# Constant rows of the attention tiles written by ScalarE and VectorE, all attention roots on VectorE, the score bound finished in thirds

## The reference

```
h = concat(tok(x), txt(x_txt))
h = h + ssm(layernorm(h))       # long convolution, gelu, linear, gelu, norm
h = h + ffn(layernorm(h))       # the last stage, the one that is changed
```

```
sx = x @ hl_w + hl_b ; q, k, v = linear maps of sx
att = softmax(q k^T * 4 + causal)               # for each n, e
mixed = sum_e gate_e * (att @ v) + resid        # gate: softmax of a linear map
hn = layernorm(mixed)                           # 36 groups of 16 per partition
hx = relu(fc1(hn)) ; hx = fc2(hx) ; y = layernorm(hx + hn)
out = y * softmax(y @ fgate)
```

## Time and profile before

| | us |
|---|---|
| time, median of 3 runs (lowest to highest) | 1520.96 (1516.12 to 1527.62) |
| the profiled execution's own time | 1521.13 |
| its span in the profile | 1519.4 |
| PE busy | 1209.2 (80%) |
| PEld busy | 612.7 (40%) |
| DVE busy | 823.8 (54%) |
| ACT busy | 830.5 (55%) |
| POOL busy | 379.0 (25%) |

### The profile page before, as it was taken

One profiled execution on the slowest core, in us unless ns is written; L12 is line 12 of the kernel. 1 busy time (PEld: TensorE's weight loads), 2 busy tenths in 40 slices (PEclk: granted clock), 3 DMA queues, 4 the chain that ended last, 5 costly groups with the idle time before them and its releaser, 6 DMA issues.

```text
span 1519.4 us, 28823 instructions
## 1 busy us (share of the span) xinstructions
PE 1209.2 (80%) x11006; PEld 612.7 (40%) x11103; DVE 823.8 (54%) x1727; ACT 830.5 (55%) x1050; POOL 379.0 (25%) x606
## 2 busy tenths in 40 slices
PE   4895558880507998899899989889989988999963
PEld 2462257760203543343343344334334434433421
DVE  4844973357622363556457457445745744654345
ACT  0231034440205587667758758766875876777750
POOL 2000040022003221432432423243242324323410
PEclk9997779995558999999999999999999999999985
DMA  9999179703139007404701910740380192065000
GB/s 158 184 186 181 14 169 202 155 1 75 49 114 135 1 13 135 64 13 88 118 1 60 134 25 14 130 76 13 79 127 1 36 140 43 13 113 86 1 17 9
DMA packets 121632, 120.66 MB, mean 79 GB/s; under 512 B 73762, under 2 KB 90417, under 8 KB 121215
## 3 DMA queue, kind: packets, MB, share of 16 engines
q1 hardware_dynamic: 117449, 118.29, 42.8%
q10 hardware_dynamic: 3733, 0.60, 0.3%
q0 software_dynamic: 320, 0.04, 0.0%
HBM read 91.05 MB, written 22.95 MB: 75 GB/s over the span
## 4 chain that ended last, share of the span: by engine, by line
PE 36%; issue 8%; ACT 8%; DMA 7%; SPq 5%; DVE 5%; POOL 5%; POOLq 0%; ACTq 0%; DVEq 0%
PE b_pso L1988 13%; PE b_pss L1964 10%; ACT b_pb L2098 7%; POOL b_stat L2121 3%; DMA qk_parts_b<-b_qs 3%; PE b_psm L2015 3%; DMA b_qop<-bound_part 3%; PE b_psm L2031 2%; PE b_psm L2045 2%; DMA b_ot<-in_c_ones 2%; POOL b_pb L2140 2%; SPq L1871 1%; PE b_psm L1947 1%; SPq L1903 1%; SPq L1904 1%
## 5 line engine op out<-in xcount | busy, mean ns | idle before, releaser
L2098 ACT ACTIVATE b_pb<-b_pss 128x1024 f32<-128x1024 f32 (+2 forms) x736 | 660.1, 934 | 334.5 <-PE b_pss L1964 255.0
L2140 POOL TENSOR_SCALAR_AFFINE_SELECT b_pb<-b_pb 128x256 f32<-128x256 f32 (+1 forms) x544 | 224.6, 431 | 719.9 <-ACT b_pb L2098 714.0
L1988 PE MATMUL b_pso<-b_pb,b_vop 128*32 128x77 f32 (+4 forms) x5376 | 375.9, 386 | 34.9 <-POOL b_pb L2140 32.7
L1964 PE MATMUL b_pss<-b_qop,b_kop 128*128 128x512 bf16 (+3 forms) x1439 | 321.7, 329 | 78.5 <-issue 53.8
L1964 PEld LDWEIGHTS b_pss<-b_qop,b_kop 128*128 128x128 bf16 x1536 | 125.0, 101 | 257.2 <-issue 108.3
L1988 PEld LDWEIGHTS b_pso<-b_pb,b_vop 128*32 128x32 f32 x5376 | 113.6, 110 | 211.7 <-issue 167.9
L2306 DVE TENSOR_TENSOR b_ofm<-b_pso,b_mk 128x512 f32<-128x512 f32 (+1 forms) x96 | 51.6, 538 | 158.2 <-PE b_pso L1988 157.3
L918 PE MATMUL psc<-tz,ub 128*64 128x128 f32 x1152 | 80.2, 284 | 45.5 <-DVE tz L1030 36.6
L2188 DVE COPY b_ot<-b_psm 128x336 f32<-128x336 f32 (+1 forms) x96 | 40.0, 417 | 104.5 <-PE b_psm L2015 104.3
L2121 POOL TENSOR_TENSOR b_stat<-b_stat,b_mh 128x18 f32<-128x18 f32 x30 | 96.0, 3216 | 0.0
L918 PEld LDWEIGHTS psc<-tz,ub 128*64 128x64 f32 x1152 | 72.0, 142 | 53.4 <-DVE ub L1026 34.2
(11 more groups left out here) (404 smaller groups left out, 1466.4 us busy)
## 6 DMA issues: line engine op xcount, KB each, us to landing
b_qop<-qk_parts_b SPq DMA_DIRECT2D x192, 144.0 KB
tz<-taps SPq DMA_DIRECT2D x64, 304.0 KB, 9.7
x<-in_x SPq DMA_DIRECT2D x16, 1024.0 KB, 13.7
qk_parts_b<-b_qs SPq DMA_DIRECT2D x16, 864.0 KB, 5.6
b_kop<-qk_parts_b SPq DMA_DIRECT2D x192, 36.0 KB
b_mk<-b_mskf SPq DMA_DIRECT2D x128, 36.0 KB, 4.9
qk_parts_b<-b_ks SPq DMA_DIRECT2D x8, 432.0 KB, 4.0
n_late<-id_d SPq DMA_DIRECT2D x1, 2400.0 KB, 9.4
```

The costliest lines, as they stand in the source:

```text
L1964: mm = pe.matmul(pss[:, u % 2, b, col:col + w], lhs, qop[:, n, e, q0:q0 + w], start=True, stop=True, skip_group_check=True)
L1988: mm = pe.matmul(pso[VW * ee:VW * (ee + 1), (3 * n + x) % 2, q0 - QT * x:q0 - QT * x + w], vop[0:r, j, n, :], pb[0:r, slot_, b, cc:cc + w] ...
L2098: nc.scalar.activation(pb[:, s % PB, 0:nb, 0:w], pss[:, s % 2, 0:nb, 0:w], ACT.Exp, scale=float(HD) ** 0.5).then_inc(exped, 1)
L2140: ins = pool.affine_select(out=v_, in_=v_, compare_op=ALU.is_ge, fill=0.0, base=0, pattern=pat, channel_multiplier=-1)
```

## The change

The constant rows. SP's 13 transfers are gone, and with them the four constants in DRAM. VectorE writes three numbers into a small tile `kons`, first thing in the stage. ScalarE copies them, broadcast along the row and read as pairs of bf16: zeros into rows 96 to 127 of head 0 of `qop` and of `kop` before its first split (`early_consts`), and after its last split of period -1 the row of -1 in `kop`, ones in all of `mk`, and the zeros of heads 1 to 3 of `qop` (`late_consts`). Each copy counts `late_ok` up by one, to 7. SP waits for the count that belongs to a head before it places that head's bound row and mask. VectorE writes the rows of `fxt`, `hx1`, `pm` and `ot` by memsets at steps 46, 49, 52 and 14 of period 0.

The roots. POOL's `root` is gone. VectorE runs `inverse_root` at the step at which POOL ran its first half (18, 31, 51, and 6 in period 0) in one piece, in every period.

The bound. Each `qnorm` is followed on VectorE by the three operations on its own third (16x384), and the block at step 78 is gone. SP waits for the third of the three.

The diff, without its unchanged lines (lines reach less far to the right than in the file):

```diff
@@ -1683,10 +1683,12 @@
...
+PAIR_ONE = 1.0 + 0x3F80 * 2.0 ** -23
+PAIR_MINUS = -(1.0 + 0xBF80 * 2.0 ** -23)
...
-def stage_ffn_bounded(nc, t, w, h2d, out, flag_d):
+def stage_ffn_bounded(nc, w, h2d, out, flag_d):
@@ -1730,6 +1732,7 @@
...
+kons = sb("b_kons", [P, 3])
...
@@ -1758,10 +1761,10 @@
...
-         "flag_ready", "bad_ready", "flag_done", "const_ready", "part0_ready", "squares_ready")
+         "flag_ready", "bad_ready", "flag_done", "const_ready", "part0_ready", "squares_ready", "consts_ready")
...
- mh_ok, xn_ok, fx_ok, flag_ready, bad_ready, flag_ok, const_ok, part0, squared) = (sem("b_" + n) for n in names)
+ mh_ok, xn_ok, fx_ok, flag_ready, bad_ready, flag_ok, const_ok, part0, squared, kons_ok) = (sem("b_" + n) for n in names)
...
@@ -1797,6 +1800,7 @@
...
+TILES = (46, 49, 52, 14)
...
@@ -1820,9 +1824,9 @@
...
-    if p <= 0:
-        return 0
-    return p * 5 - 3 if p == B else p * 5 - 2
+    if isinstance(p, int) and p <= 0:
+        return 1 + p
+    return p * 5 - 2 if isinstance(p, int) and p == B else p * 5 - 1
...
@@ -1858,19 +1862,6 @@
...
-                many = lambda name, r, n: rows(t[name][0:n], r.stop - r.start)
-                pad, low = slice(KB_, P), slice(KT, KB_)
-                sp.dma_start(qop[pad].bitcast(F32).rearrange("k n e q -> k (n e q)"), many("c_zeros", pad, NH * NE * LP // 2)).then_inc(late_ok, 16)
-                sp.dma_start(kop[pad].bitcast(F32).rearrange("k n q -> k (n q)"), many("c_zeros", pad, NH * LP // 2)).then_inc(late_ok, 16)
-                sp.dma_start(kop[low].bitcast(F32).rearrange("k n q -> k (n q)"), many("c_minus", low, NH * LP // 2)).then_inc(late_ok, 16)
-                for e in range(NE):
-                    free_ = slice(32 * e + HD, 32 * e + 32)
-                    sp.dma_start(mk[free_].bitcast(F32).rearrange("k n q -> k (n q)"), many("c_pairs", free_, NH * LP // 2)).then_inc(late_ok, 16)
-                for x in (fxt, hx1):
-                    sp.dma_start(x[D + 1:P], many("c_zeros", slice(D + 1, P), LP)).then_inc(late_ok, 16)
-                    sp.dma_start(x[D:D + 1], many("c_ones", slice(D, D + 1), LP)).then_inc(late_ok, 16)
-                sp.dma_start(pm[D:P], many("c_zeros", slice(D, P), LP)).then_inc(late_ok, 16)
-                sp.dma_start(ot[LAST:P, :, NA - 1, :], many("c_ones", slice(LAST, P), NH * MIXW).rearrange("p (n w) -> p n w", n=NH)).then_inc(late_ok, 16)
...
@@ -1888,7 +1879,7 @@
...
-                sp.wait_ge(bound_ok, c + 1)
+                sp.wait_ge(bound_ok, 3 * c + 3)
...
@@ -1905,12 +1896,17 @@
...
+                    if not att:
+                        sp.wait_ge(late_ok, 1 if n == 0 else 4 + n)
+                        sp.sem_inc(sp_passed, 1)
...
+                    else:
+                        sp.wait_ge(late_ok, 4)
...
@@ -2054,7 +2050,7 @@
...
-                pe.wait_ge(late_ok, 16 * 13)
+                pe.wait_ge(late_ok, 7)
...
@@ -2070,6 +2066,22 @@
...
+        zero_q = lambda n: nc.scalar.copy(qop[KT:P, n].rearrange("k e q -> k (e q)").bitcast(F32), bcast(kons[KT:P, 0], NE * LP // 2)).then_inc(late_ok, 1)
+
+        def early_consts():
+
+            act.wait_ge(kons_ok, 3)
+            zero_q(0)
+            nc.scalar.copy(kop[KT:P].rearrange("k n q -> k (n q)").bitcast(F32), bcast(kons[KT:P, 0], NH * LP // 2)).then_inc(late_ok, 1)
+
+        def late_consts():
+
+            act.wait_ge(late_ok, 2)
+            nc.scalar.copy(kop[KT:KB_].rearrange("k n q -> k (n q)").bitcast(F32), bcast(kons[KT:KB_, 1], NH * LP // 2)).then_inc(late_ok, 1)
+            nc.scalar.copy(mk[:].rearrange("k n q -> k (n q)").bitcast(F32), bcast(kons[:, 2], NH * LP // 2)).then_inc(late_ok, 1)
+            for n in range(1, NH):
+                zero_q(n)
+
...
@@ -2099,6 +2111,8 @@
...
+                        if p < 0 and c == FEATS[-1]:
+                            late_consts()
...
@@ -2108,17 +2122,13 @@
...
+        early_consts()
...
-
-        def root(c, st, lo, hi):
-
-            pool.wait_ge(var, c)
-            pool.tensor_tensor(st[:, 3, lo:hi], st[:, 2, lo:hi], mh[:, lo:hi], ALU.pow).then_inc(rstd, 1)
...
@@ -2141,15 +2151,9 @@
...
-            norms = 0
...
-                for when, st, n, on_ in ((FXNORM, stat, NA * NH, prev), (RNORM, stat, NA * NH, att and not prev), (XNORM, statx, NA, pro), (LASTNORM, stat, NA * NH, prev)):
-                    if on_ and att and s in when[1]:
-                        i, m = when[1].index(s), n // len(when[1])
-                        norms += i == 0
-                        root(variances(p) + norms, st, i * m, (i + 1) * m)
...
@@ -2162,6 +2166,8 @@
...
+        for i, x in enumerate((0.0, PAIR_MINUS, PAIR_ONE)):
+            nc.vector.memset(kons[:, i:i + 1], x).then_inc(kons_ok, 1)
...
@@ -2211,7 +2217,13 @@
...
-                give(ts(bound[:, c * FB:(c + 1) * FB], bank()[0:HE, 0:FB], kmax[:, 3:4], ROUNDING, ALU.mult, ALU.mult))
+                third = bound[:, c * FB:(c + 1) * FB]
+                give(ts(third, bank()[0:HE, 0:FB], kmax[:, 3:4], ROUNDING, ALU.mult, ALU.mult))
+                v.wait_ge(free, base + k[0] + 2)
+                bits = third.bitcast(I32)
+                ch.step(ts(bits, bits, 1, None, ALU.logical_shift_right))
+                ch.step(ts(bits, bits, HALF_BIAS, None, ALU.add))
+                ts(mt[:, c * FB:(c + 1) * FB], third, -SHIFT / float(HD) ** 0.5, None, ALU.add).then_inc(bound_ok, 1)
...
@@ -2291,7 +2303,7 @@
...
-            roots0 = norms_before(p)
+            norms = 0
...
@@ -2329,17 +2341,25 @@
...
-                    v.wait_ge(rstd, roots0 + 2)
...
-                    if att:
-                        v.wait_ge(rstd, roots0 + 2)
+                    tt(fx[:], mix[:], bcast(stat[:, 3], HD), ALU.mult).then_inc(fx_ok, 1)
+                for when, st, n, on_ in ((FXNORM, stat, NA * NH, prev), (RNORM, stat, NA * NH, att and not prev), (XNORM, statx, NA, pro and att), (LASTNORM, stat, NA * NH, prev)):
+                    if on_ and s == when[1][0]:
+                        norms += 1
+                        v.wait_ge(var, variances(p) + norms)
+                        inverse_root(nc, ch, st[:, 3, 0:n], st[:, 2, 0:n], st[:, 1, 0:n])
+                if att and not prev and s in TILES:
+                    i = TILES.index(s)
+                    if i < 2:
+                        ch.step(nc.vector.memset((fxt, hx1)[i][D:P], 0.0))
+                        ch.done(nc.vector.memset((fxt, hx1)[i][D:D + 1], 1.0))
+                    elif i == 2:
+                        ch.done(nc.vector.memset(pm[D:P], 0.0))
...
-                        v.wait_ge(var, variances(p) + 1)
-                        inverse_root(nc, ch, stat[:, 3], stat[:, 2], stat[:, 1])
-                    tt(fx[:], mix[:], bcast(stat[:, 3], HD), ALU.mult).then_inc(fx_ok, 1)
+                        ch.done(nc.vector.memset(ot[D:P, :, NA - 1, :], 1.0))
...
@@ -2349,7 +2369,6 @@
...
-                    v.wait_ge(rstd, roots0 + 3)
...
@@ -2365,12 +2384,6 @@
...
-                    if s == BOUND:
-                        v.wait_ge(free, base + k[0] + 2)
-                        bits = bound[:].bitcast(I32)
-                        ch.step(ts(bits, bits, 1, None, ALU.logical_shift_right))
-                        ch.step(ts(bits, bits, HALF_BIAS, None, ALU.add))
-                        ts(mt[:], bound[:], -SHIFT / float(HD) ** 0.5, None, ALU.add).then_inc(bound_ok, 1)
...
@@ -2384,11 +2397,6 @@
...
-                    if att:
-                        v.wait_ge(rstd, roots0 + 4 + pro)
-                    else:
-                        v.wait_ge(var, variances(p) + 2)
-                        inverse_root(nc, ch, stat[:, 3], stat[:, 2], stat[:, 1])
...
@@ -2428,7 +2436,7 @@
...
-stage_ffn_bounded(nc, t, w, h2d, out, flag_d)
+stage_ffn_bounded(nc, w, h2d, out, flag_d)
...
@@ -2463,10 +2471,6 @@
...
-"c_zeros": np.zeros(NH * NE * LP // 2),
-"c_ones": np.ones(LP),
-"c_minus": np.full(NH * LP // 2, np.uint32(0xBF80BF80)).view(np.float32),
-"c_pairs": np.full(NH * LP // 2, np.uint32(0x3F803F80)).view(np.float32),
...
```

## The result

| | before | after |
|---|---|---|
| time, median (lowest to highest, runs) | 1518.54 (1511.33 to 1527.62, 4) | 1470.14 (1463.23 to 1471.95, 4) |
| the profiled execution's own time | 1521.13 | 1463.23 |
| its span | 1519.4 | 1461.5 |

The ratio is 0.967, with a 95% interval of 0.962 to 0.973: the change takes 48 us, where 49 were forecast. Six more runs of the changed kernel beside eleven of the one before gave 1469.36 against 1521.62, ratio 0.965 [0.962, 0.969].

The account below looks back on a forecast made before the run. PE's own work bounds periods with attention; in period -1 SP's backed-up queue holds PE. Gains of 44.7 (gap), -0.6 (period 0), 3.0 (periods 1 to 6) and 2.0 (period 7), 49.1 us off 1521.13, give 1472 us, range 1458 to 1486.

Parts of the forecast that it names:

- The gap: Period -1, PE idle 53.6 us before its first score: without the 13 transfers the score comes 44.7 us earlier (42.9 to 45.7).
- The rival in which the queue stays clogged: SP's queue in period -1: `h4` loads crawl without the constants too, spill 15.5 us later; 1487 to 1490, chance 0.05.
- The root off POOL: Step 18, periods 1 to 7: PE's 2.04 us stand for POOL's masks goes completely, gaining 2.0 us in each.
- The losses at steps 51 and 64: VectorE delays PE: root at 51 costs 0.7 us in periods 1 to 6, bound's third at 64 0.8 in periods 0 to 6.
- Period 0: First period with attention: 0.7 us gained, 0.5 and 0.8 lost, so 0.6 us longer in sum.
- The memset pair at step 46: Period 0, VectorE, ahead of the accumulator and mask job PE wants at step 49: costs PE 0.5 us (0 to 2).
- the root at step 31: VectorE's root of 9 groups, at most 2.7 us, in front of one `fc1` emptying: costs nothing, at worst 1 us.
- The `h4` norm: Period 0, VectorE: PE's 0.73 us wait at step 13 for POOL's root and the product behind it; 0.7 us gained.
- Masks held back by the roots: Step 18: VectorE's root delays POOL's masks by 1.4 us in each of seven periods, 9.8 in all; 1482, chance 0.12.
- VectorE's queue leaks more: VectorE's in-order queue: one further root exposed to PE in each of periods 1 to 6, 16 us; 1488, chance 0.12.
- The spared stalls are worth more: No loss at steps 51 and 64, and 45.7 us for PE's wait before its first score; 1461, chance 0.15.
- Slower: VectorE's queue, periods 0 to 7: extra work exposed in full, some 88 us against 44.7; 1564, chance 0.01.

## Why the prediction came out right, step by step

**The gap, forecast 44.7, was 44.8.** Every link held, and two small errors in it cancel. From the stage's start to the spill I had 28.6 us, the trace 29.0; from the spill to the first score I took 18.2, between 17.2 and 20.0, and it was 17.6. The copies took 2.11 us (I had at most 2.3) and, with the table load behind them, ended 7.8 us ahead of the first score (I had 7.6). The doubtful point was the queue: I left the `h4` loads the whole of their 21.96 us; they took 3.32, which gained nothing, since the spill waits for VectorE. The rival in which the queue stays clogged fell. Had they taken the 21.96, SP would have been through them at 391.5, still ahead of the spill at 398.09. The sign that I had named, a first score at 419 to 422 us, was missed in its letter: it came at 415.69, since the stage itself began 4.1 us earlier. From the stage's start it is 46.6, where the sign means 46 to 49.

**The root off POOL, forecast 2.0 in each period, was 2.4.** PE's job that turns `fx` comes 2.43 us earlier against the period's start in the middle periods: 2.04 of it is the wait of the earlier trace rows, 0.26 the wait for `b_fx` behind it. (In period 2 only 2.1 of it last beyond that job.) The run with the first root back on POOL puts the root's price higher, at 3.0 us a period, the clock behind such waits included. PE's timeline of period 2 has it without a wait:

```profile
703.65 0.66 PE L1943 MATMUL b_psm<-w_ident,b_fx 128*128 128x128 f32 x4
```

**The losses at steps 51 and 64, forecast 0.7 and 0.8, were 0.7 and 1.0.** Both waits are where the prediction put them, in PE's timeline of period 2:

```profile
752.22 1.12 PE L2011 MATMUL b_psm<-w_mixer,b_ofm 128*128 128x84 f32 x8 [0.65 <-DVE b_ofm L2318]
...
772.34 0.91 PE L2027 MATMUL b_psm<-b_xt,w_all 128*128 128x384 f32 x2 [0.60 <-DVE b_rq L2233]
```

The third's 1.0 is worked out from the start times of PE's jobs against the period's start, before and after: the 0.60 of the wait and 0.4 in small shifts behind it. So a period gains 0.6 to 0.7 us (period 2 less), where I had 0.5, some 4 of the 11.7 us in six periods. The rest is PE's clock (the last section) and the waits for the bound's row at the ends of these periods (10.1 us before, 7.7 after), neither of which the sum had. Part of this is luck of the profiled execution: in the second profile of the changed kernel periods 1 to 6 took 758.6 us, 8.0 less than before. With the bound in one block the time fell by 9.6 us, where I had 5.6 for the thirds and seven times 1.0 would be 7; the profiles bear out their direction and leave the size open.

**Period 0 was mis-sized: forecast 0.6 us longer, it was 4.2.** Two terms failed. The memset pair at step 46 I took at 0.5 us (0 to 2); the jobs behind it are 1.75 us later. And the root at step 31 I took at nothing, "at worst 1 us", looking only at the `fc1` emptying of the periods with features and an output block; in period 0 it stands in front of copies of `b_xt` that PE waits for, and the jobs behind are 1.1 us later. VectorE's timeline shows the root, the copies and the pair:

```profile
462.99 0.15 DVE L55 TENSOR_SCALAR b_statx<-b_statx 128x9 int32<-128x9 int32 x1
...
465.22 0.17 DVE L63 TENSOR_TENSOR b_statx<-b_statx 128x9 f32<-128x9 f32 x1
465.42 0.88 DVE L2199 COPY b_xt<-b_psm 64x512 f32<-64x512 f32 x2
...
485.73 1.02 DVE L2357 MEMSET b_fxt<- 64x1152 f32 x1 [0.30 <-issue]
487.04 1.02 DVE L2358 MEMSET b_fxt<- 1x1152 f32 x1 [0.30 <-DVE b_fxt L2357]
```

and PE's timeline the two waits:

```profile
466.36 1.06 PE L2016 MATMUL b_psm<-w_all,b_xt 128*128 128x16 f32 x8 [1.06 <-DVE b_xt L2199]
...
490.48 0.34 PE L2011 MATMUL b_psm<-w_mixer,b_ofm 128*77 128x84 f32 x2 [1.70 <-DVE b_mx L2213]
```

The `h4` norm's 0.7 us I had as gained was 0.9. The thirds added 1.0 and the landing of the bound's row 0.6. That makes 3.6 of the 4.2; of the rest, PE's first jobs were 0.3 late already, ahead of all these steps. A sign that I had named for being wrong, periods longer than before, so came up in period 0 (and in period 2, by 0.8 us). With both steps moved (and the block), period 0 took 128.2 us.

**So the total is right in part by errors that cancel**: in the profiled pair, 3.6 us too little lost in period 0 and 8.7 too little gained in periods 1 to 6. By parts the errors are smaller, and cancel again. The constants alone gave 47 to 48 us, for which the forecast has 44.7 less 0.5 for the memsets, 44.2. Roots and thirds gave 1 to 4, for which it has 14.0 (2.0 in seven periods) and 0.7 (the `h4` norm) less 4.2 (step 51) and 5.6 (thirds), 4.9. So I had some 3 us too little for the one and 1 to 4 too much for the other. Of the 3, one or two are in the gap, which fell by 46.4 and 45.3 us in the two profiles of the constants alone; the rest has no place that the profiles name.

**The rivals.** *Masks held back by the roots* did not happen: POOL's masks beside the root at step 18 took at most 0.45 us instead of 0.41, and PE's waits for them fell to 14.6 us in total. That the two engines get in each other's way, as the Trainium skill has it ("SBUF — State Buffer", Who interferes with whom), agrees with the trace, but it was VectorE that stretched. VectorE's timeline has two steps of the root in period 2 that took 0.32 us each, where the same steps in period 8, with no mask beside them, took 0.20 and 0.18. The second of them has a single input, so that more than steps with two inputs stretch beside a mask. The root runs from 694.11 to 697.33, 3.2 us in place of the 2.7 of the earlier trace rows, and behind it the wait that still covers it:

```profile
695.87 0.32 DVE L61 SCALAR_TENSOR_TENSOR b_stat<-b_stat 128x36 f32<-128x36 f32 x1
...
696.78 0.32 DVE L62 TENSOR_SCALAR b_stat<-b_stat 128x36 f32<-128x36 f32 x1
...
699.43 0.69 DVE L2318 TENSOR_TENSOR b_ofm<-b_pso,b_mk 128x512 f32<-128x512 f32 x1 [2.10 <-PE b_pso L1984]
```

*VectorE's queue leaks more* was true in period 0 alone. *The spared stalls are worth more* was true of the gap's end and of the root (2.4, not 2.0), but its premise, no loss at steps 51 and 64, was wrong. *Slower* never came near: of 63.5 us more on VectorE some 14 reached PE (6 x 0.7, 7 x 1.0 and 2.9 in period 0).

## What to carry to other kernels

Look at the row count of every transfer in a queue that something urgent stands behind: cutting transfers of 31, 63 and 51 rows into pieces of 16 and 15, 48 and 15, and 48 and 3 gave 41 of the 48 us that the whole change gave. Work that an in-order engine takes over goes step by step into its own idle slots, and each period that lacks some jobs (the first one here) has to be read by itself; moving five of them by one to nine places gave, with the bound in one block, 34.5 us more. A swap whose parts gain and lose has to be run apart: here the thirds of the bound and the places of three other steps ate nearly all that the first root gave.

## What the runs showed of the hardware

**A transfer's row count decides how many DMA engines are busy with it.** With transfers of 31 rows (1116 KB and 279 KB) in the queue the 16 engines were 7% busy at 28 GB/s in the 10 us window, and 13% busy at 43 GB/s from 390 to 442 us; with 16 + 15 rows, and the others cut likewise, they were 91% busy at 111 GB/s. The Trainium skill ("DMA: Bandwidth & Descriptors", Why a DMA increments its semaphore by 16 and not by 1) says that a transfer is spread over the largest number of engines up to 16 that divides the slowest dimension of both its sides, by which 31 rows go to one engine, and 16 and 15 rows to 16 and 15. The trace agrees: 0.07 of 16 engines is about one of them. An estimate from these numbers fits too: at 28 GB/s the two transfers' 1395 KB take 51 us, most of the 69 us from the first transfer's issue to the last one's landing. No run cuts the 31 rows alone, so that the share of the 63 and 51 rows is not known.

**Issuing into a backed-up queue takes long on SP.** The four `h4` loads took 21.96 us to issue behind the slow transfers and 3.32 with none ahead of them. But they took 19.66 us behind the transfers cut in pieces as well, where all 16 engines were busy: it is what still stands in the queue that stretches an issue, not only how few engines work on it. What the cut changed is when the queue was free: the last load was issued 27.5 us after the stage's start and not 70.2.

**PE's granted clock fell behind some of its waits inside otherwise busy stretches.** In the kernel before, windows on either side of a wait of 2.04 us in period 3, and then around the same wait in period 2, where nothing fell:

```profile
871.00:873.40 2.40, 2.35 (x43) 1.42 (x43) 0.51 (x1) 1.48 (x3) 2.40 (x2) 1.00 1.10 133
876.00:879.00 3.00, 2.87 (x13) 2.31 (x14) 1.00 (x3) 0.89 (x1) 0.62 (x2) 0.50 0.55 125
747.00:750.00 3.00, 1.29 (x35) 0.67 (x34) 0.29 (x2) 2.16 (x3) 3.00 (x2) 1.00 0.56 84
751.00:754.00 3.00, 3.00 (x26) 1.73 (x27) 1.60 (x2) 1.94 (x2) 1.18 (x4) 1.00 1.01 214
```

1.00 is 2.4 GHz and 0.50 is 1.2. Two of the seven root waits of the kernel before were followed by it, and three of its waits for the bound's row (2.6, 2.65 and 3.35 us). The same seven waits of 2.04 to 2.08 us stand in four more profiles and were followed by it four and three times (the constants alone, twice), five times (the first root back on POOL) and five times (the transfers in pieces): 19 of 35 in all. In the changed kernel's first profile only the wait of 3.20 us at the end of period 0 was, within the attention; in its second, three waits for the bound's row (3.19, 1.84 and 2.06 us) and one other. So a stall that a change spares, or makes, is worth more than its length on some of its occasions, and the total cannot be had from the lengths alone. With the bound in one block it also fell in period 0, behind the 1.06 us wait of step 34, and stayed low for some 10 us:

```profile
462.00:465.00 3.00, 1.98 (x13) 0.38 (x11) 2.61 (x13) 2.41 (x3) 0.00 (x0) 1.00 0.00 0
466.00:472.00 6.00, 6.00 (x24) 2.82 (x25) 1.29 (x4) 1.59 (x2) 0.00 (x0) 0.51 0.00 0
```

The one other fall in the changed kernel's second profile was of this kind, with a period 0 of 136.0 us against 133.3. What decides between a wait that is followed by it and one that is not stays open.
